# Cross-attention and top-k expert layer on one core: two-bit threshold search, joined ranks, and a new order of the steps around the experts

## What is computed

```python
x = x + _L0_xattn_ref(_layernorm(x), mask, ctx_1024, mask2, ...)     # tanh over 4096 x 77 x 256
# then, on the layernorm of that x, 8 experts of capacity T / E = 512:
logits = jnp.einsum('gsd,de->gse', x, gate)
probs = jax.nn.softmax(logits, axis=-1)
scores, token_idx = jax.lax.top_k(flat_probs, k=capacity)            # for each expert its 512 best of 4096 tokens
tok = flat_x[token_idx]
h = jax.nn.gelu(jnp.einsum('ecd,edh->ech', tok, W1) + b1[:, None, :])
out_tok = jnp.einsum('ech,ehd->ecd', h, W2) + b2[:, None, :]
routed = jnp.zeros_like(flat_x).at[token_idx.reshape(-1)].add((out_tok * scores[..., None]).reshape(...))
shared = jax.nn.gelu(x @ Ws1 + bs1) @ Ws2 + bs2
x = x + routed + shared
```

## Time and profile before

| | before |
|---|---|
| median of three runs | 1005.41 us (1004.53 to 1007.21) |
| the profiled execution | 1006.52 us, of which the span 1004.4 us |
| TensorE matmul (PE) busy | 823.5 us, 82% |
| VectorE (DVE) busy | 736.8 us, 73% |
| ScalarE (ACT) busy | 755.9 us, 75% |
| GpSimd (POOL) busy | 172.2 us, 17% |
| mean granted clock of TensorE | 0.948 of full speed |

### The profile page before, as it was taken

One profiled execution on the slowest core, in us unless ns is written; L12 is line 12 of the kernel. 1 busy time (PEld: TensorE's weight loads), 2 busy tenths in 40 slices (PEclk: granted clock), 3 DMA queues, 4 the chain that ended last, 5 costly groups with the idle time before them and its releaser, 6 DMA issues.

```text
span 1004.4 us, 14303 instructions
## 1 busy us (share of the span) xinstructions
PE 823.5 (82%) x5471; PEld 476.0 (47%) x5471; DVE 736.8 (73%) x1589; ACT 755.9 (75%) x558; POOL 172.2 (17%) x278
## 2 busy tenths in 40 slices
PE   4765775559999876999997799983797899999993
PEld 2211221124454432545442354452565788888883
DVE  4898897998785888888588866945667476676630
ACT  1999999998999897999898799952111466666662
POOL 1100110120120030101003000103201144444422
PEclk9899999978999987999998899997898899999997
DMA  7000000010001011000001000004200244444421
GB/s 256 1 1 1 1 1 1 1 42 2 1 1 43 1 35 50 2 1 22 1 1 43 22 1 22 1 22 131 80 21 12 67 116 120 124 124 126 126 31 21
DMA packets 32517, 41.94 MB, mean 42 GB/s; under 512 B 2365, under 2 KB 29121, under 8 KB 32449
## 3 DMA queue, kind: packets, MB, share of 16 engines
q1 hardware_dynamic: 26307, 32.66, 9.8%
q0 software_dynamic: 6144, 8.39, 4.9%
HBM read 28.46 MB, written 12.58 MB: 41 GB/s over the span
## 4 chain that ended last, share of the span: by engine, by line
PE 50%; ACT 24%; DVE 14%; issue 7%; DMA 1%; POOL 1%; SPq 0%; ACTq 0%; DVEq 0%
ACT z L829 18%; PE bank L668 12%; PE bank L779 9%; PE bank L722 8%; PE bank L803 8%; PE bank L711 6%; DVE z L1108 6%; ACT z L825 4%; PE bank L644 2%; PE bank L603 2%; DVE onehot L1398 1%; PE bank L735 1%; DVE xn L1032 1%; ACT u L854 1%; DMA w_raw<-in_L_ffn_W_dram 1%
## 5 line engine op out<-in xcount | busy, mean ns | idle before, releaser
L829 ACT ACTIVATE z<-z 128x3072 f32<-128x3072 f32 (+4 forms) x157 | 497.2, 3190 | 22.7 <-DVE z L1108 22.7
L1108 DVE TENSOR_SCALAR z<-feat,txt_bias 128x1024 f32<-128x1024 f32 (+1 forms) x678 | 392.0, 649 | 43.2 <-PE bank L668 43.0
L668 PE MATMUL bank<-z,window 128*32 128x512 f32 x2464 | 316.2, 622 | 76.2 <-ACT z L829 76.0
L668 PEld LDWEIGHTS bank<-z,window 128*32 128x32 f32 x2464 | 71.5, 113 | 275.3 <-issue 148.1
L722 PE MATMUL bank<-ws_sb,u 128*128 128x256 f32 x512 | 134.6, 403 | 10.7 <-DVE x_ring L1293 6.3
L722 PEld LDWEIGHTS bank<-ws_sb,u 128*128 128x128 f32 x512 | 95.5, 198 | 52.1 <-issue 34.2
L854 ACT ACTIVATE u<-bank,vec 128x512 f32<-128x512 f32 x64 | 43.5, 681 | 94.3 <-PE bank L711 94.2
L711 PE MATMUL bank<-tr,ws_s 128*128 128x512 f32 x384 | 112.4, 430 | 0.0
L779 PE MATMUL bank<-xg_s,w_s 128*128 128x512 f32 x384 | 101.8, 402 | 2.1 <-DVE xg_s L1424 2.1
L803 PE MATMUL bank<-w_s,hid_s 128*128 128x256 f32 x768 | 101.4, 281 | 0.0
L803 PEld LDWEIGHTS bank<-w_s,hid_s 128*128 128x128 f32 x768 | 98.4, 188 | 5.5
(11 more groups left out here) (179 smaller groups left out, 646.7 us busy)
## 6 DMA issues: line engine op xcount, KB each, us to landing
w_raw<-in_L_ffn_W_dram SPq DMA_DIRECT2D x16, 1024.0 KB, 5.1
x_ring<-in_x_dram SPq DMA_DIRECT2D x8, 512.0 KB, 7.8
xn_dram<-xn SPq DMA_DIRECT2D x8, 512.0 KB, 2.9
out_dram<-x_ring SPq DMA_DIRECT2D x8, 512.0 KB, 2.9
u<-in_L_ffn_Ws_dram SPq DMA_DIRECT2D x1, 1024.0 KB, 9.0
ws_sb<-in_L_ffn_Ws_dram SPq DMA_DIRECT2D x1, 1024.0 KB, 11.4
xg<-xn_dram,idx POOLq DMA_INDIRECT x32
out_dram<-y,idx POOLq DMA_INDIRECT x32
```

The lines of the kernel that those rows point to most:

```text
L668: ins = e.matmul(sums[v][32 * r:32 * r + 32, :], window[:, c, 31 - k:63 - k], z[:, n % ZB, at_piece:at_piece + TOK], start=(v, r) not in b ...
L829: e.activation(part, part, ACT.Tanh).then_inc(signal(*step), 1)
L1108: ins = e.tensor_scalar(z[:, n % ZB, i * width:(i + 1) * width], feat_of(units, c), bias_of(units, t, c), None, ALU.add)
```

## The change

- Threshold search: two bits in a step. `count` makes three comparisons with the three candidates 1, 2 and 3 in the digit, `total` sums three columns, `decide` turns the three answers into the digit by exclusive or and makes three new candidates. 15 steps take the place of 30.
- Ranks: tokens above the threshold and tokens equal to it are scanned in one round; one group of sums gives the three offsets. `above`, `total_above`, `left` and one round go.
- The first expert's weights: their loads are issued right after the last attention block; `split_hi` is done in eight quarters, 128 x 512 each, on ScalarE before the search, and each `split_lo` stands between the `total` and the `decide` of one search step. The four `whole` pieces of unit 7 stand there too.
- Unit 5's `down_end` on VectorE moves from ahead of `y_norm` of unit 7 to behind it. `exp_again` (the exp table load) moves ahead of `y_norm`, `router` of unit 6 moves behind `y_turned` of unit 7, two pieces of filler move from the stretch before the search into it, and the third Newton multiplication is fused.
- `vals` is built in two parts: tiles 0 to 23 while the last attention blocks run, the rest after unit 7's `router`. `pick` is cleared at the start.
- The biases are 8 short rows on partitions 0 to 7 and 32 to 39, loaded at the start and split on VectorE in attention.
- 90 one-element fills of GpSimd make two tables of constants for the search (step `earlier`, early in attention).
- The second expert's list: only `mark 1` and its first two `mark_slots` stay ahead of the experts, and wait for the second indirect load of the first gather; the rest stands in the first expert's steps m = 0 to 2, and the third expert's list moves to m = 3 to 6. In the first expert the transposes of the next one's tokens move from m = 2 to m = 5. For later experts `fold`, `folded` and `gather` now stand ahead of the second split of w2.

The diff, cut to its core:

```diff
+    at_slots(0, (8,), [[("split_b2",)]])
...
+    at_slots(base, (5,), [[("values", 0, NT - 2 * J)]])
...
-    order += [*end[0], *end[1], *end[2], ("att_exp", vb), ("logits_exp", va), *end[4], *end[5], *end[6], ("router", va), *end[7]]
-    fill(5)
-    for steps in (end[8], end[9]):
-        order += steps
+    ended = []
+
+    def fill_chain(n):
+
+        for _ in range(n):
+            steps = filler.pop(0)
+            ended.extend(step for step in steps if step[0] in BY_VECTOR)
+            order.extend(step for step in steps if step[0] not in BY_VECTOR)
+
+    order += [*end[0], *end[1], ("load_w1", 0), ("load_w2", 0), *end[2], ("att_exp", vb), ("logits_exp", va)]
+    fill_chain(1)
+    order += [*end[4], *end[5], *end[6], *end[7]]
+    fill_chain(3)
+    first_split = [("split_hi", name, 0, h) for name in ("w1", "w2") for h in range(PIECES[0])]
+    beside = [[("split_lo", *step[1:])] for step in first_split] + [[step] for step in end[12]]
+    order += [("exp_again",), *end[8], *end[9], *first_split, *ended]
     fill(1)
-    order += [*end[10], *end[11], *end[13]]
-    fill(2)
-    order += [("exp_again",), *end[12], *end[14], *end[15], ("logits_exp", vb)]
+    order += [*end[10], *end[11], *end[13], ("router", va)]
     fill(1)
-    order += [("router", vb)]
-
-    order += [("values",), ("load_w1", 0), ("load_w2", 0)]
-    order += [step for name in ("w1", "w2") for h in range(2) for step in split(name, 0, h)]
-    order += [("load_w1", 1), ("load_w2", 1), ("b2_rows",), ("load_b2",), ("split_b2",)]
+    order += [*end[14], *end[15], ("logits_exp", vb), ("router", vb), ("values", NT - 2 * J, NT)]
     for hf in range(NH):
         order += [("probs_turn", hf), ("probs_out", hf)]
-    for bit in range(FIRST_BIT, -1, -1):
+    order += [("load_w1", 1), ("load_w2", 1)]
+    for bit in range(THRESHOLD_BITS - DIGIT, -1, -DIGIT):
         order += [("count", bit), ("total", bit)]
-        fill()
-        order.append(("decide", bit))
-    order += [("above",), ("total_above",)]
-    fill()
-    order.append(("left",))
-    for name in ("equal", "chosen"):
-        order += [("ranks", name), ("rank_total", name)]
-        fill()
-        order.append(("ranked", name))
+        fill(2)
+        order += [*(beside.pop(0) if beside else []), ("decide", bit)]
+    order += [("masks",), ("ranks",), ("rank_total",)]
+    fill(2)
+    order += [("offsets",), ("ranked",)]
     order.append(("slots_turn",))
     fill()
     order.append(("slots",))
-    for ex in range(2):
-        order.append(("mark", ex))
-        fill(LIST_FILL[ex])
-        for q in range(4):
-            order += [("mark_slots", ex, q), ("list", ex, q)]
-        order += [("listed", ex), ("fold", ex), ("folded", ex), ("gather", ex)]
+    order.append(("mark", 0))
+    fill(LIST_FILL)
+    for q in range(4):
+        order += [("mark_slots", 0, q), ("list", 0, q)]
+        fill(1 if q < 2 else 0)
+    order += [("listed", 0), ("fold", 0), ("folded", 0), ("gather", 0), ("mark", 1), ("mark_slots", 1, 0), ("mark_slots", 1, 1)]
...
+    def listing(ex, *parts):
+        steps = []
+        for part in parts:
+            if part == "fold":
+                steps += [("fold", ex), ("folded", ex), ("gather", ex)]
+            elif part == "list":
+                steps += [*(("list", ex, q) for q in range(4)), ("listed", ex)]
+            elif part == "mark":
+                steps.append(("mark", ex))
+            else:
+                steps.append(("mark_slots", ex, part))
+        return steps if ex < E else []
+    def beside_experts(ex, m):
+        steps, after = [], ex + 1 < E
+        at_split = {0: ("w1", 0), 1: ("w1", 1), 4: ("w2", 0), 5: ("w2", 1)}
+        if ex == 0:
+            if m < 3:
+                steps += listing(1, *((2,), (3, "list"), ("fold",))[m])
+            elif m < 7:
+                steps += listing(2, *(("mark", 0), (1, 2), (3, "list"), ("fold",))[m - 3])
+        elif m < 6:
+            steps += listing(ex + 2, *(("mark",), (0,), (1,), (2, 3), ("list",), ("fold",))[m])
+        if after and m in at_split:
+            steps += split(at_split[m][0], ex + 1, at_split[m][1])
+        if m == (5 if ex == 0 else 2) and after:
+            steps += turn_gathered(ex + 1)
+        if ex + 2 < E and m in (1, 5):
+            steps.append(("load_w1" if m == 1 else "load_w2", ex + 2))
+        return steps
...
                     if ex == 0:
-                        e.wait_ge(*done("router", vb))
                         e.wait_ge(*done("tanh", LAST - 1))
                         e.wait_ge(*done("rho", LAST - 1))
-                        e.wait_ge(*done("y_turned", vb, C - 1))
-                        e.wait_ge(xn2_stored[vb], 16)
                     else:
...
-                    if kind == "total":
-                        e.wait_ge(*done("count", *args))
-                    else:
-                        e.wait_ge(*done("above"))
-                    e.matmul(take(TOTAL)[:, 0:1], same_expert[:], cnt[:, 0:1], start=True, stop=True).then_inc(signal(*step), 1)
+                elif kind == "total":
+                    bit, = args
+                    e.wait_ge(*done("count", bit))
+                    e.matmul(take(TOTAL)[:, 0:CANDIDATES], same_expert[:], cnt[:], start=True, stop=True).then_inc(signal(*step), 1)
                 elif kind == "rank_total":
-                    e.wait_ge(*done("ranks", *args))
+                    e.wait_ge(*done("ranks"))
                     e.wait_ge(*done("earlier"))
                     dst = take(TOTAL)
-                    e.matmul(dst[:, 0:1], earlier_tile[:], cnt[:, 2:3], start=True, stop=True)
-                    e.matmul(dst[:, 1:2], same_expert[:], cnt[:, 2:3], start=True, stop=False)
-                    e.matmul(dst[:, 1:2], earlier_tile[:], cnt[:, 3:4], start=False, stop=True).then_inc(signal(*step), 1)
+                    flat = scan[:].rearrange("p w k -> p (w k)")
+                    above, equal = flat[:, NH * P - 1:NH * P], flat[:, (NH + 1) * P - 1:(NH + 1) * P]
+                    e.matmul(dst[:, 0:1 + NH], earlier_tile[:], flat[:, NH * P - 1:2 * NH * P:P], start=True, stop=False)
+                    e.matmul(dst[:, 1:1 + NH], same_expert[:], above.broadcast_to([P, NH]), start=False, stop=False)
+                    e.matmul(dst[:, NH:NH + 1], same_expert[:], equal, start=False, stop=True).then_inc(signal(*step), 1)
...
-                    e.wait_ge(gathered[ex % 2], 16 * A * (ex // 2 + 1))
+                    if ex:
+                        e.wait_ge(gathered[ex % 2], 16 * A * (ex // 2 + ex % 2))
+                    else:
+                        for a in range(A):
+                            e.wait_ge(first_gathered[a], 16)
...
+                    e.memset(cur[:], 0)
+                    for place in range(THRESHOLD_BITS // DIGIT):
+                        for i in range(CANDIDATES):
+                            e.memset(steps_of[:, place, i:i + 1], (i + 1) << (place * DIGIT))
+                            ins = e.memset(turns_of[:, place, i:i + 1], (i + 1 ^ i) << (place * DIGIT))
+                    ins.then_inc(signal(*step), 1)
...
-                        link(e.tensor_tensor(ra[:], ra[:], ve[:], ALU.mult))
+                        link(e.scalar_tensor_tensor(out=ra[:], in0=ra[:], scalar=-0.5, in1=ve[:], op0=ALU.mult, op1=ALU.mult))
                         e.wait_ge(vector_link, linked)
-                        link(e.tensor_scalar(ra[:], ra[:], -0.5, 1.5, ALU.mult, ALU.add))
-                        e.wait_ge(vector_link, linked)
-                        link(e.tensor_tensor(ry, ra[:], ry, ALU.mult))
+                        link(e.scalar_tensor_tensor(out=ry, in0=ra[:], scalar=1.5, in1=ry, op0=ALU.add, op1=ALU.mult))
...
+                    for i, passed in enumerate((gt[:], eq[:], scan[:, 0, :])):
+                        ins = e.tensor_scalar(passed, pt[:], asked[:, i:i + 1].bitcast(F32), None, ALU.is_ge, ALU.add,
+                                              accum_out=cnt[:, i:i + 1])
...
-                    e.tensor_scalar(okbit[:, 0:1], tot_ps[:, 0:1], float(CAP), float(1 << bit),
-                                    ALU.is_ge, ALU.mult).then_inc(signal(*step), 1)
+
+                    e.scalar_tensor_tensor(out=reached[:], in0=tot_ps[:, 0:CANDIDATES], scalar=float(CAP),
+                                           in1=turns_of[:, bit // DIGIT, :], op0=ALU.is_ge, op1=ALU.mult).then_inc(signal(*step), 1)
                     e.wait_ge(*done("decide", bit))
+                    e.tensor_tensor(digit[:], reached[:, 0:1], reached[:, 1:2], ALU.bitwise_xor)
+                    link(e.tensor_tensor(cur[:], reached[:, 2:3], cur[:], ALU.bitwise_xor))
+                    e.wait_ge(vector_link, linked)
+                    link(e.tensor_tensor(cur[:], digit[:], cur[:], ALU.bitwise_xor))
+                    e.wait_ge(vector_link, linked)
                     if bit:
```

(7 more changed lines are left out.)

261 lines of the change are left out of this document (107 added, 154 removed).

## The result

The changed kernel takes **987.62 us** in the median (986.77 to 988.92, 4 runs); beside it on the same chip the kernel before took 1004.97 us (1003.24 to 1007.21). The ratio is 0.983, interval 0.980 to 0.985. The profiled execution took 988.92 us, with a span of 987.2 us against 1004.4 us.

A forecast was written before the change was run, and what follows sets the result against it. Attention and experts were taken as full, the routing stretch as bound by chains of small waiting steps; 13.6 + 3.2 + 2.2 + 4.5 - 7.6 = 15.9 us off 1006.5 gave 990.6, median 989.5 us, forecast range 985 to 994 (chance 0.60).

The forecast's parts named there:

- Up to the first count: From attention's end to the search's first count: early loads and hidden splits bring it to 691.0 us, 13.6 us gained.
- rival (c): Before the first count: loads come late or ScalarE's split quarters hold up the exp; 1000.5 us, chance 0.04.
- The search: First count to last `decide`: 15 two-bit steps set by VectorE take 46.7 us instead of 49.9, 3.2 us gained.
- Rival (b): Search steps take 3.3 us because reads and exclusive ors don't overlap: 7.5 us more, 997 us, chance 0.16.
- (d): TensorE is granted 1.2 GHz in the search because it idles each step: 24 us more, 1013 us, chance 0.03.
- To the slots: Last `decide` to the slots: 6.4 us instead of 8.63, 2.2 us gained.
- To the first `e_up`: First indirect load to first `e_up`: 10.4 us instead of 14.9, 4.5 us gained; only 2 if TensorE is cold again.
- The first expert: First `e_up` of expert 0 to expert 1's: TensorE waits for VectorE's list work; 31.4 us instead of 23.85, 7.6 lost.
- steps 4 and 5: Way to the experts, 4.5 us gained, and first expert, 7.6 us lost, from moving the second expert's list.
- Rival (a): VectorE keeps up in the first expert, only the gap at m = 5 stays: about 7 us better, 982, chance 0.15.
- Elsewhere: In attention: fills and early bias split cost nothing to 1 us; `vals` part one nothing, at most 4.3 us.

The follow-up runs named there:

- late loads: Changed kernel, but the first expert's weights loaded behind the last router step again and split whole ahead of the search: 998.44 us, ratio 0.995.
- the changed kernel once more: The changed kernel unaltered, run again beside three of the follow-up kernels: 988.17 us, ratio 0.986 against the kernel before.
- the list in the gap: Changed kernel, with the second expert's last two marks and list in VectorE's gap during the first expert's first `up`: 981.12 us, ratio 0.978.
- the last wait attacked: Changed kernel with early constants, the second list in VectorE's gap, its fold and gather ahead of the first down, transposes earlier: 977.08 us, ratio 0.975.

## Why the prediction was right, and where it was off

The time was foretold at 989.5 us and is 987.6. Of 17.2 us in the span, 15.9 were foretold, but four rows of the table were off by more than a microsecond (the first count, the search, attention, the end), and they partly cancel. That the total came within 2 us is in part luck.

1. **Up to the first count: right.** 20.97 us from `rho_sb` instead of 35.74. The loads and splits are 11 us of it (late loads), `down_end` about 1 (the experiment with it ahead); the other 2.7 (Newton, the exp table, two pieces of filler) no run takes apart. The first count came at 691.52 us, foretold at 691.0, but from an attention that ended 1.65 us late: the step itself was 1.1 us better than I had it. The exp did not stand behind the splits, rival (c) is out.
2. **The search: the direction right, the size half.** I had 46.7 us, it took 42.8. The term that was too large is the comparison: 0.49 us each, where the rows show 0.40, since the read runs beside the next comparison. I had 0.41 as the lower bound and took 0.49 as the nearest row. The step is 0.47 + 0.84 + 1.35 = 2.66 us, the last being two spacings of 0.40 and the 0.54 from a comparison's start to `total`. The 0.15 us for a split's overhang were 0.04 (2.66 against 2.62 in steps without one). The first step, at a granted clock of 0.63, took 3.98 us and not 5.1. The step with `down_end` was 1.4 us over, for 1.6 foretold. Against all that, the step behind it was 1.5 us over, at a clock of 0.50 that I had not foreseen; in the executions where it did not fall, the search took 41.4 us, and I was off by more. Rival (b), longer steps, is out, and so is (d): the clock was 1.00 from 700 to 720 us.
By the Trainium skill (TensorE: Matmul & The Clock Gate, part 1) activity releases the clock; the trace agrees in the whole of the search but for two steps, yet the same wait of 2.1 us was followed by 1.2 GHz in five executions and by 2.4 GHz in four, so the rule gives no number for it here.
3. **To the slots: right,** 6.20 us for 6.4.
4. **To the first `e_up`: right,** 10.60 us for 10.4, with the granted clock at 1.00 from 750 to 760 us. In the first three `up` behind it the clock was 0.71, which belongs to the next stretch.
5. **The first expert: the mechanism right, the size within 1.3 us.** 32.39 us for 31.4, but 1.6 us of it is the clock in the first three `up` (5.97 us against 4.35); in the changed kernel once more, where the clock was 1.00, the stretch took 30.07. The stalls stand where they were foretold: 1.54 us at m = 1 (1.35), 2.58 at m = 5 (3.3), 1.46 behind the transposes (1.5 to 2); the first two came out the same in the second execution. What I left out is that TensorE is at 1.2 GHz behind the last two: the transposes take 1.94 us (1.06 in the second execution), and the second expert's first `e_up` 2.90 instead of 1.63 (2.90 in the second execution too), which is the 1.3 us lost "to the end". With that the edit to which steps 4 and 5 belong lost 5.5 us in this pair of profiles (4.31 - 8.54 - 1.3), where I had 3.1. The experiment that puts the list back ahead gives 4 us on the whole. Rival (a), VectorE keeps up, is false for this order and nearly true for another: with the list in the gap and the last wait attacked it was 26.7 us from bias to bias, against 35.4 and, with the list ahead, 25.1.
6. **Elsewhere: the term that failed.** I put the fills and the bias split at nothing to 1 us "beside ScalarE's tanh", and `vals` at nothing because the adds are blocks ahead. Attention ended 1.65 us later in this pair of profiles. ScalarE waited 1.67 + 0.19 us behind the fills and 0.9 us more than before behind the two casts at 541 us; that makes 2.8 us, and the three kernels with both moved ended attention 2.5 us earlier than the eight without. The kernel before has one profile only (668.90 us), so how much of this attention really lost against it is known no better than 1.5 to 3.4 us. The four later `vals` operations (642 us) stretched seven adds to 4.65 us from 2.85 and cost nothing: there the cover held. So "blocks ahead" is true at some blocks and false at others, where ScalarE waits for the adds anyway (the 0.19 us in the row of before was the sign of it), and I didn't look at the block.
By the Trainium skill (GPSIMD Engine Reference, section 8, Key points) GpSimd shares SBUF interfaces with VectorE and gets in its way in some forms of instruction. I had put that beside the sum; the traces agree with it, with four adds at 5.21 us beside one-element fills and 2.74 without. Of the 4.3 us that I gave as the most for `vals`, 0.9 came.

## What to carry to other kernels

A step that is moved into a full stretch costs what its queue neighbours wait, not what it takes: look for the engine's own gap first (3.15 us here held two marks; the list begun there made the kernel 6.5 us shorter than with it in the steps behind), and then for who is the next to wait for the step's result, as the gather was. Small writes by GpSimd were not free beside VectorE here, even with one element each: put them where VectorE's output is not awaited. And where two spacings are possible for an instruction in line, take the one that the rows show between two starts, not the sum of lengths. Before a difference of 1 or 2 us between two profiles is explained, look at how far two executions of the same kernel lie apart: here 1.75 us at the end of attention and 2.3 in the first expert.

## What the hardware did that I had not expected

- 91 one-element fills on GpSimd, 0.03 us apart, nearly doubled four fp32 adds of VectorE beside them: 5.21 us against 2.74 (4.13 us in the kernel with the list ahead). Two casts did 2.97 against 2.07 for three, and four operations 4.65 against 2.85 for seven.
- The read of an accumulator (0.08 us) cost nothing where another comparison followed: spacing 0.40 us in line.
- Issues of an indirect load take 0.95 us alone, but 1.57, 1.47 and 1.44 us in the first expert of the kernel with the list in the gap, while VectorE's marks and splits ran. No run takes these away, so that they are the cause is not shown. The transposes that wait for the rows began 10.7 us behind the first issue (769.11 to 779.85).
- The granted clock behind one and the same wait (2.1 us, one step of the search) fell to 0.50 in five executions and stayed at 1.00 in four. Where it fell, the search was 1.3 us longer, about half of what an interval here can tell.
